# A decoder layer on one core: the first group's projections and the last group's attention in other PSUM banks, and new queue orders

## What is computed

```python
x = x + _L0_attn_ref(_layernorm(x), ...)    # a Mamba mixer
x = x + _L0_xattn_ref(_layernorm(x), ctx_2048, ..., 64)   # banded attention over the features
x = x + _L0_ffn_ref(_layernorm(x), ...)     # 8 experts, the best 2
```

```python
# mixer: I = 1024 channels, N = 16 states, R = 128, K = 4 taps
h_in, gate = split(x @ in_proj_w.T)
u = silu(causal_depthwise_conv(h_in, conv_w) + conv_b)
ts, Bm, Cm = split(u @ x_proj_w.T)
dt = softplus(ts @ dt_proj_w.T + dt_proj_b)
h[t] = exp(dt * A) * h[t-1] + dt * u * Bm        # a scan over the 128 tokens, per channel and state
y = (sum_n h * Cm + D * u) * silu(gate)
return y @ out_proj_w.T
```

```python
# attention: the 512 features are the positions, the 128 tokens the channels: 8 heads of 16
q, k, v = split(x_T @ w_in.T + b_in)
attn = softmax(where(|q_pos - k_pos| <= 64, q k / 4, -inf))
out = w_ct applied to (relu(attn v @ w_out.T + b_out) * context) + b_ct
```

```python
# experts
gate = softmax(x @ router.T) kept for the top 2
out = sum_e gate_e * (silu(x @ down_e.T) @ up_e.T)
```

## Time and profile before

| | |
|---|---|
| median of 3 runs | 4977.84 us (4977.36 to 4978.13) |
| profiled execution, its own time | 4972.81 us |
| its span | 4971.0 us |
| mean granted TensorE clock | 0.982 |
| TensorE busy | 4574.1 us (92%) |
| VectorE busy | 4434.0 us (89%) |
| ScalarE busy | 4400.9 us (89%) |
| GpSimd busy | 4196.7 us (84%) |

### The profile page before, as it was taken

The page is one execution under the profiler, slowest core; times in us unless marked ns, Lnnn a source line. Parts: engine busy times, 40 slices in busy tenths (PEclk is TensorE's granted clock), DMA queues, the critical chain, the costliest instruction groups (busy, mean ns, idle before and its releaser), DMA issues.

```text
span 4971.0 us, 143017 instructions
## 1 busy us (share of the span) xinstructions
PE 4574.1 (92%) x52548; PEld 3357.0 (68%) x52548; DVE 4434.0 (89%) x6051; ACT 4400.9 (89%) x9310; POOL 4196.7 (84%) x3467
## 2 busy tenths in 40 slices
PE   4799999999999999999999999999999999999976
PEld 3666666766766776776776767676666677666653
DVE  2899999999999999999999999999999999999961
ACT  3798999999999999999999999999999999999862
POOL 2988898888898888898888898888889888888860
PEclk8899999999999999999999999999999999999996
DMA  3212222212222221222221222221222221122100
GB/s 124 79 46 71 76 78 78 82 54 67 76 78 78 82 69 52 82 76 78 78 82 38 85 77 75 81 82 40 80 76 78 78 82 56 64 77 77 65 14 7
DMA packets 119316, 350.46 MB, mean 71 GB/s; under 512 B 18688, under 2 KB 19456, under 8 KB 118528
## 3 DMA queue, kind: packets, MB, share of 16 engines
q1 hardware_dynamic: 118656, 341.51, 20.7%
HBM read 323.64 MB, written 17.83 MB: 69 GB/s over the span
## 4 chain that ended last, share of the span: by engine, by line
PE 47%; DVE 18%; POOL 12%; issue 11%; ACT 8%; DMA 2%; DVEq 1%; SPq 0%; ACTq 0%; POOLq 0%
PE ps L1204 9%; PE ps L1156 9%; POOL ring L320 8%; PE ps L1224 5%; DVE ring L1542 5%; POOL ring L329 4%; DVE ps L1542 4%; PE ps L1100 4%; PE ps L1111 3%; DVE nmax L1564 3%; ACT ps L498 3%; PE ps L1072 3%; PE ps L1233 2%; DMA x_new<-in_x 2%; PE ps L1034 1%
## 5 line engine op out<-in xcount | busy, mean ns | idle before, releaser
L320 POOL TENSOR_TENSOR ring<-du,bc 128x512 f32<-128x512 f32 x2048 | 2579.3, 1277 | 486.6 <-PE ps L1156 368.0
L498 ACT ACTIVATE ps<-delta,a_neg 128x254 f32<-128x254 f32 x4096 | 1771.6, 468 | 39.5 <-DVE ring L1542 31.3
L329 POOL TENSOR_TENSOR ring<-ring,bc 128x512 f32<-128x512 f32 x1280 | 1621.6, 1277 | 110.7 <-DVE ring L1542 109.5
L1542 DVE TENSOR_TENSOR_SCAN ring<-ps,ring 128x512 f32<-128x512 f32 x1280 | 1542.5, 1213 | 143.9 <-ACT ps L498 123.9
L1156 PE MATMUL ps<-ident,ring 128*128 128x128 f32 x8192 | 1073.3, 276 | 70.2 <-POOL ring L329 65.5
L1156 PEld LDWEIGHTS ps<-ident,ring 128*128 128x128 f32 x8192 | 925.0, 142 | 179.1 <-issue 99.6
L1542 DVE TENSOR_TENSOR_SCAN ps<-ps,ring 128x512 f32<-128x512 f32 x768 | 933.5, 1215 | 48.8 <-ACT ps L498 39.2
L1526 DVE TENSOR_TENSOR ring<-ps,bc 128x512 f32<-128x512 f32 x768 | 526.4, 685 | 19.0
L657 ACT ACTIVATE probs_mem<-ps 128x768 f32<-128x768 f32 (+1 forms) x512 | 449.8, 912 | 66.8 <-PE ps L1100 63.4
L1224 PE MATMUL ps<-w_in,xt_a 128*128 128x256 f32 x2048 | 484.2, 391 | 20.9 <-ACT delta L550 12.0
L1204 PE MATMUL ps<-xt_a,w_in 128*128 128x256 f32 x2048 | 475.9, 386 | 8.5 <-DVE hc L1646 4.1
(11 more groups left out here) (140 smaller groups left out, 6381.0 us busy)
## 6 DMA issues: line engine op xcount, KB each, us to landing
w_in<-in_w_in SPq DMA_DIRECT2D x256, 512.0 KB, 3.6
bc<-bc_rows SPq DMA_DIRECT2D x256, 512.0 KB, 5.5
x_new<-in_x SPq DMA_DIRECT2D x32, 512.0 KB, 6.7
x_res<-in_x SPq DMA_DIRECT2D x32, 512.0 KB, 6.2
enc<-in_ctx SPq DMA_DIRECT2D x64, 256.0 KB, 3.2
out<-x_att SPq DMA_DIRECT2D x32, 512.0 KB, 3.2
w_outp<-in_w_outp SPq DMA_DIRECT2D x1, 2048.0 KB, 7.9
bc_rows<-bc_sb SPq DMA_DIRECT2D x128, 8.0 KB, 1.5
```

Of the source, the lines that this page charges most:

```text
L320: nc.gpsimd.tensor_tensor(ring[:, s % RING, :].rearrange("p (n t) -> p n t", n=2), du[:, q % 2, (ic % 2) * NT:(ic % 2 + 1) * NT].rearrange ...
L329: nc.gpsimd.tensor_tensor(ring[:, s % RING, :], ring[:, s % RING, :], bc[:, s % RS, 2:4, :].rearrange("p a t -> p (a t)"), ALU.mult).then_ ...
L498: nc.scalar.activation(ps[:, bank("step", s), (n % 2) * NT:(n % 2 + 1) * NT].rearrange("p (b t) -> p b t", b=GB)[:, :, 1:T], delta[:, ic, ...
L1542: nc.vector.tensor_tensor_scan(state, ps[:, bank("step", s), :], ring[:, s % RING, :], 0.0, ALU.mult, ALU.add).then_inc(h_done, 1)
```

## The change

1. **First group.** A function `prep_bank(j, use, q)` picks the PSUM bank of a projection. For group 0 the h projections use banks 4 to 7, ts bank 4, the B and C rows bank 5, dt banks 6, 7 and 4, and the gates bank 3; for every other group it is bank 3 as before. The waits of `h_in`, `gate_in` and `dt_in` that guarded the one bank go for group 0.
2. **Last group.** A tuple `Lane` names everything that a row's attention uses: its first bank, its buffers and its semaphores. The second row of group 31 gets a lane of its own with banks 0 to 3 and buffers in `bc`, `hc0` and `xt_a`. GpSimd clears three of its buffers with memsets (`second_lane`), and `context` for it waits for the last gate projection.
3. **Orders.** Iteration -1 becomes `first_iteration`, iterations 32 and 33 become `last_iteration`, each with an order of its own on GpSimd, ScalarE, TensorE and VectorE. The order within `iteration`, which all other iterations run, changes too, on the same four engines; the operations in it are the same.

The core of the diff, first the banks and the lanes:

```diff
+        def prep_bank(j, use, q=0):
+
+            if not first(j):
+                return PS_B
+            return {"h": PS_ATT + q, "ts": PS_ATT, "bc": PS_ATT + 1, "dt": (PS_ATT + 2, PS_ATT + 3, PS_ATT, PS_B)[q]}[use]
...
+        def lane(g, b):
+
+            return lanes[1 if isinstance(g, int) and g == NG and b == 1 else 0]
...
+            def second_lane(g):
...
+                nc.gpsimd.memset(L.v_aug[:, :, :, DH + 1:32], 0.0).then_inc(spare_set, 1)
+                nc.gpsimd.memset(L.v_aug[:, :, :, DH:DH + 1], 1.0).then_inc(spare_set, 1)
+                nc.gpsimd.memset(L.nmax, 0.0).then_inc(spare_set, 1)
...
             def h_in(j, q, cur):
 
                 slot, k = ((1, 0), (0, 0), (0, 1), (0, 2))[q]
-                if q < 2:
+                if first(j):
+                    pass
+                elif q < 2:
...
             def gate_in(j, q, cur):
 
                 slot, k = ((1, 1), (1, 2), (1, 3), (0, 3))[q]
-                if q < 2:
+                if first(j) and q < 3:
+                    pe.wait_ge(xt_done["a"], 2)
+                    reached(pe, gate_done, q)
+                elif q < 2:
```

The start of TensorE's and of VectorE's list in `iteration`:

```diff
             def iteration(g, cur, nxt, p1, p2):
                 j = g + 1
-                if p1:
+                if cur:
+                    dt_in(g, 3, cur)
+                if p1:
+                    y_sum(g - 1, 63)
                     out_proj(g - 1, 0, 0, 4)
-                    y_sum(g - 1, 63)
-                if cur:
-                    dt_in(g, 3, cur)
+                if cur:
+                    gate_in(g, 3, cur)
...
             def iteration(g, cur, nxt, p1, p2):
                 j = g + 1
+                if p2:
+                    shift("e", g - 2, 0)
+                if p1:
+                    y_step(g - 1, 7)
                 if cur:
                     scan(g, 0)
                     scan(g, 1)
```

More of the change, by code:

```diff
@@ L2 @@
 from concourse import mybir
+from collections import namedtuple
 from contextlib import ExitStack
@@ L761, in iteration @@
                 if p1:
+                    attention(g, p2, 0, "qk", 3)
                     attention(g, p2, 0, "v")
+                if cur:
+                    decays(g, 18)
+                    soft_exp(g, 1)
+                    decays(g, 19)
+                if nxt:
+                    x_norm(j, 0)
+                    x_norm(j, 1)
+                if cur:
+                    decays(g, 20)
                 if nxt:
@@ L959, in iteration, with first_iteration @@
                     variance("e", g - 1, 1)
-            iteration(-1, False, True, False, False)
+            def first_iteration(g):
+                j = g + 1
+                total(j, 0)
+                total(j, 1)
+                squares("a", g + 1, 0)
+                squares("a", g + 1, 1)
+                variance("a", g + 1, 0)
+                variance("a", g + 1, 1)
+                x_norm(j, 0)
+                x_norm(j, 1)
+                x_copy(j, 0)
+                x_copy(j, 1)
+                gate_raw(j, 0)
+                tap3(j, 0)
+                tap3(j, 1)
+                tap3(j, 2)
+                u_silu(j, 0)
+                u_silu(j, 1)
+                gate_raw(j, 1)
+                tap3(j, 3)
+                gate_silu(j, 0)
+                u_silu(j, 2)
+                u_silu(j, 3)
+                ts_copy(j)
+                skip_term(j, 0)
+                gate_raw(j, 2)
+                step_size(j, 0)
+                step_size(j, 1)
+                bc_rows(j)
+                soft_exp(j, 0)
+                soft_one(j, 0)
+                soft_ln(j, 0)
+                skip_term(j, 1)
+                soft_back(j, 0)
+                step_size(j, 2)
@@ L1245, in dt_in @@
             def dt_in(j, q, cur):
-                if q == 0:
+                if first(j) and q < 3:
+                    pass
+                elif q == 0:
                     if cur:
@@ L1429, in iteration @@
                 if p1:
+                    attention(g, p2, 1, "st", 2)
+                if cur:
+                    y_sum(g, 49)
+                if nxt:
+                    bc_in_rows(j)
+                if p1:
                     attention(g, p2, 1, "st", 3)
                 if cur:
+                    y_turn(g, 5, nxt)
                     y_sum(g, 51)
                 if nxt:
-                    bc_in_rows(j)
+                    dt_in(j, 0, cur)
                 if cur:
-                    y_turn(g, 5, nxt)
+                    y_sum(g, 53)
                 if p1:
@@ L1662, in iteration @@
                 if cur:
+                    times_c(g, 1)
+                    scan(g, 2)
                     scan(g, 3)
-                if p1:
-                    y_step(g - 1, 7)
-                if cur:
                     scan(g, 4)
@@ L1702, in iteration @@
                 if cur:
-                    scan(g, 12)
+                    times_c(g, 12)
+                    scan(g, 13)
+                    y_step(g, 0)
                 if p2:
@@ L1716, in iteration @@
                 if cur:
+                    times_c(g, 15)
+                    scan(g, 16)
+                if nxt:
+                    shift("a", g + 1, 0)
+                if cur:
                     scan(g, 17)
                     times_c(g, 17)
+                    scan(g, 18)
                 if p1:
                     attention(g, 0, "max", 0)
+                if nxt:
+                    shift("a", g + 1, 1)
                 if cur:
-                    scan(g, 18)
+                    y_step(g, 1)
                     scan(g, 19)
@@ L1800, in iteration @@
                 if p1:
+                    attention(g, 0, "x2")
+                if cur:
+                    times_c(g, 39)
+                if nxt:
+                    conv(j, 5)
+                if p1:
                     attention(g, 1, "max", 0)
                 if cur:
-                    times_c(g, 39)
                     scan(g, 40)
+                    scan(g, 41)
                 if p1:
@@ L1813, in iteration @@
                 if cur:
-                    scan(g, 43)
                     scan(g, 44)
+                    times_c(g, 44)
                 if p1:
@@ L1818, in iteration @@
                 if cur:
-                    times_c(g, 44)
+                    scan(g, 45)
                     y_step(g, 4)
-                    scan(g, 45)
                 if p1:
@@ L1847, in iteration @@
                     scan(g, 57)
+                    times_c(g, 57)
+                    scan(g, 58)
                 if p1:
@@ L1850, in iteration @@
                 if cur:
-                    times_c(g, 57)
-                    scan(g, 58)
+                    scan(g, 59)
                     y_step(g, 6)
```

867 lines of the change are left out of this document (527 added, 340 removed).

## The result

The changed kernel takes **4892.8 us** (4890.1 to 4893.9) against 4977.6 us for the kernel before beside it: 0.983 of it, 95% interval 0.981 to 0.985. The prediction was 4890, 0.982. The profiled execution has a span of 4888.2 us, 82.8 less than before.

What follows compares the result with a forecast made beforehand. TensorE, 95% busy, was taken to fill the loop, with serial chains at both ends. Span 4971.0 - 24 - 49 - 15 = 4883; as time 4977.84 - 88 = 4890 us, range 4845 to 4940.

Steps and rivals of the forecast that it cites:

- Sum: Whole kernel: gains at the head, the tail and in the loop together take 88 us off, to 4890 us.
- part 3: Loop body: reordered queues on four engines change a group by -0.5 us, times 30 groups -15 us.
- Part 1: First group's projections: own banks bring the first scan from 101.58 to 77.1 us, gain 24 us.
- Part 2: Last group's attention rows side by side: 63 us for 111, gain 48, plus 0.9 from unqueued steps.
- the walk through the engines: Last attention: new order stepped through four engines with full-clock durations from the trace, giving 63 us.
- my full clock: Last attention: TensorE's granted clock above 0.9, near the loop's 1.00, for the gain of 48 us.
- the middle sum of 31: Last attention: a gain near 31 us if the clock swings, between 14 at low level and 48 at full clock.
- (a): Loop, score and st blocks: more filler where TensorE waited, -2 to -3 us a group.
- (b): Group boundary: later du, first decay and TensorE waits for dt_in and y_sum, +1 to +2 us a group.
- (c): Loop, ScalarE: one table load less a group, 1.28 us of ScalarE, taken as 0 for the time.
- Rival E: Group head: y_step(7) bars VectorE's scans, dt_in(3) bars y_sum(63); +3.5 us a group, 5010 us, slower than before; chance 0.06.

Runs made afterwards that it cites:

- experiment 6: The changed kernel with SyncE issuing the second group's x_new load ahead of the first group's B and C rows: 4895.3 us.
- experiment 3: The kernel before with both new ends, the order inside the loop left old: 4907.1 us, ratio 0.986.
- experiment 1: The kernel before with only the first group's new banks and the first iteration's new order: 4953.9 us, ratio 0.996.
- experiment 7: The changed kernel with one y_sum moved ahead of the second st of each attention row: 4893.2 us.
- experiment 5: The changed kernel plus eight matmuls in the tail whose results nobody reads: 4888.5 us.
- experiment 4: The kernel before with only the new order of the loop, also used at both ends; banks and ends old: 4966.1 us, ratio 0.998.
- experiment 11: The changed kernel with the old order in the middle of the group on four engines, GpSimd's rstd kept behind one product: 4946.9 us, ratio 0.994.
- experiment 10: The changed kernel with the old order in the middle of the group on four engines, GpSimd's rstd behind three products: 5002.7 us, ratio 1.004.
- experiment 12: The changed kernel with only GpSimd's rstd moved back behind three products: 4949.2 us, ratio 0.994.
- experiment 8: The changed kernel with the old boundary order on TensorE, VectorE and ScalarE's end, step_size(3) left in its new place: 4942.4 us, ratio 0.993.

## Why the prediction was right, and where it was lucky

**Sum.** 88 us predicted, 82.8 of span and 84.8 by the medians measured: 4890 for 4892.8. That it is so near is luck in part, since part 3 holds a slip of addition.

**Part 1, the head, right.** First scan 77.1 predicted, 76.36 measured; in the nine other kernels with the same head it lies between 76.30 and 77.98 (78.50 with the early x_new of experiment 6). The weight slots hold the pace as costed. Not seen was who stands behind: x_new of the second group, issued behind the B and C rows and landing late, and GpSimd, which paces the first group anyway. So the 24 us at the first scan aren't all kept: by the first out the head gains 19 to 20 with the old order of the loop (experiments 3 and 1) and 21 to 25 with the new (experiments 7 and 5, and the changed kernel). The loop's order alone brings nothing by then (419.88 in experiment 4). I had taken the start of a chain for the gain; the first out is the milestone that counts.

**Part 2, the tail, 49 predicted, 42.0 measured.** The mechanism was right (63 us predicted, 67.5 measured, for 111.0), and two terms were mis-sized, the first mostly and the second wholly by the clock. In the attention the clock was 0.55 from 4830 to 4840, and the st took 1.88 there. Experiment 7 has the same order at 1.00 throughout: 64.2 us. So the clock accounts for 3.3 of the 4.5 us, and the walk through the engines was 1.2 us short. The st blocks' pauses were the same 1.9 us in both traces, so they alone did not decide whether the clock fell; over the eleven traces with the new tail the attention took 64.2 to 69.6 us. And the experts' chain was "unchanged" in the prediction at 20.9, but its router group had 2.08 us before and 3.42 after; the chain took 22.2 at 0.50. Experiment 5 shows that this is the clock and not the work: 16.0 at 1.00. The old tail's chain had lost some 5 us to the clock as well, and the prediction left that gain aside. The Trainium skill (TensorE: Matmul & The Clock Gate, A second HAM failure mode) has a kernel whose clock swings as it cycles through PSUM banks with short pauses. The trace agrees in part: the new tail swung, but at a mean of 0.93, which is far nearer to my full clock than to the middle sum of 31 that I had set beside it.

**Part 3, the loop, -15 predicted, -15.7 measured, and -14.3 by the medians.** The number is right; the path to it is half right, and the number itself rests on a slip. (a) is -2 to -3 and (b) +1 to +2, so their sum runs from -2 to 0 and not from -2.0 to +1.0. Its middle is -1.0 a group, -30 us, and the forecast would have been 4875. The -0.5 that was written down is what was measured.
- (a) fillers, -2 to -3 a group: with the new boundary the new middle measures -1.8 (experiment 11 against the changed kernel), a little under the range. The waits went as costed: 1.6 us a group of the maxima's (predicted 1.8), o's and GpSimd's entirely, and the st's came to 1.9 (56.5/29.5) where I had put two of 0.9. But experiment 7 shows that filling a wait of TensorE is not in itself a gain, with the old boundary the same middle is worth nothing (+0.1 to +0.3), and up to 1.1 of the 1.8 may be the place of `mixer_add`. So the terms "such a wait goes, so much is gained" were not what carried it. What did is open between the engines' queues: the chain that ended last passes through GpSimd for 22% of the span now and 12% before, through VectorE for 10% and 18%, which is a reading of the chain and no test.
- (b) the boundary, +1 to +2: with the old middle it measures +1.3 to +1.4, as predicted. With the new middle it measures -0.6 to -0.75: the sign turns. Of the steps named, one held: du about 1 us later. GpSimd's wait for du went from 1.4 to 2.7 us a group, and to 2.3 in experiment 11. The waits of TensorE were wrong. It was to wait 1.4 for dt_in and 0.5 for the y_sum; in the changed kernel it waits for neither, because the gate copy comes no later than the y_sum before it ends, and in experiment 11, where the +1.3 was measured, 0.3 for each. The late step on VectorE is the shift, queued ahead of the scans and waiting for GpSimd's rstd, which itself stands behind a product that waits for du. I had passed it over and put y_step(7) there.
- (c) one table load less: ScalarE has 9280 instructions for 9310, 30 less, and nothing in the runs prices it alone. The Trainium skill (ScalarE: Activation LUTs, What ACT_TABLE_LOAD costs) adds a drain to a load. The trace of the changed kernel has none either: the load of 1981.09 takes 1.28 and its activation starts at 1982.39.
- Adding (a) and (b) gave the right sum along one of two paths, old/old to new boundary to new middle (+1.4, -1.9). Along the other the terms are +0.1 and -0.6. That the parts may not be additive was not in the prediction at all.

**Rival E**, slower by a barred VectorE at the head of the group, was given 0.06 and +3.5 us a group with 4905 + 105 = 5010 as its time. It didn't happen, but experiment 10 is that case: 5002.7, 3.2 us a group above experiment 3. Its kind of mechanism was right, a step in front of VectorE's scans, but the bar was the shift and not y_step, and it is 1.8 of the 3.2 us: that much comes back in experiment 11. What spoke against it in the prediction (TensorE ran through) did not exclude it; what excluded it was the place of rstd in GpSimd's list and the middle that goes with it (experiments 11 and 12). The first stood in the diff and not in my text.

**Not settled:** why the new middle is worth 1.8 us only behind the new boundary. The wait of `mixer_add` is a candidate for up to 1.1 of it. Moving that step alone, or splitting the middle by engine, would tell; these twelve runs don't.

## What to carry to other kernels

In this kernel, where every engine runs a fixed list, an order was worth something only with the other lists that it was made for. So price a change in one list by what each of its steps waits for in the others. Before moving a step ahead of a bottleneck's work, look up the position of its supplier in the supplier's queue; here two products ahead of a 0.7 us step cost 56 us. A half of a change that is tested alone can have a wait that neither kernel has (experiments 8 and 11): look for it in the trace before you read the time. And a wait of the busiest engine is not a price: fill it and see which wait comes in its place.

## What the hardware showed unexpectedly

The clock of a serial tail could be bought back with work that nobody needs. Eight matmuls of 0.9 us each (4.45 us for five, 2.82 for three) kept the granted clock at 1.00 (2.4 GHz) through the last 16 us, where it had been 0.50 (1.2 GHz), and the stretch took 16.0 us. Without them it took 20.6 in three and 22.2 in seven traces with the same last iteration, the changed kernel's among the seven.

Without such work the same code met different clocks in different executions. The last attention took 64.2 us at 1.00 (experiment 7), 67.5 at 0.93 (the changed kernel) and 69.6 at 0.88 (experiment 10), with the same order in its last iteration and the same pauses of 1.9 us in front of its st blocks. So a single trace places this tail to some 5 us only.
